# A decoder layer on one core: where the softmax's reciprocal and scaled copy stand in the order, when gathered rows are summed and normed, and how many constants' products run at the start

## The reference, cut to what matters

```python
def reference(x, ctx_1024, ...):            # x, ctx: (8, 256, 128)
    x = _layernorm(x + attention(x))        # sparse attention, 8 heads
    x = _layernorm(x + retention(x, ctx, ctx))   # 16 heads of 8
    return _layernorm(x + top2_moe(x))      # 8 experts, 128 -> 512 -> 128

# attention: index scores I choose 96 keys for each query (64 local, 32 chosen)
    _, idx = jax.lax.top_k(I, 96)
    scores = (einsum(q_c, k_c[idx]) + einsum(q_r, key_r)) * scale
    attn = softmax(scores)
    out = einsum('bhlk,bhlkd->bhld', attn, v[idx]) @ W_out
# retention: out = ((rot(Q) @ rot(K).T) * decay_mask) @ V
# moe:       hidden = relu(x @ w1 + b1);  all = hidden @ w2 + b2
#            y = sum over the two chosen experts of prob * all
```

## Time and profile before

| what | value |
|---|---|
| median of 3 executions | 669.03 us (668.65 to 680.7) |
| the profiled execution, its own time | 668.53 us |
| its span in the trace | 666.7 us |
| mean granted TensorE clock, of full speed | 0.961 |
| busy, share of the span | PE 88%, DVE 65%, ACT 61%, POOL 40% |

### The profile page before, as it was taken

The page is one execution under the profiler, slowest core; times in us unless marked ns, Lnnn a source line. Parts: engine busy times, 40 slices in busy tenths (PEclk is TensorE's granted clock), DMA queues, the critical chain, the costliest instruction groups (busy, mean ns, idle before and its releaser), DMA issues.

```text
span 666.7 us, 22154 instructions
## 1 busy us (share of the span) xinstructions
PE 585.0 (88%) x8225; PEld 439.7 (66%) x8225; DVE 432.2 (65%) x1618; ACT 406.9 (61%) x1381; POOL 268.0 (40%) x428
## 2 busy tenths in 40 slices
PE   5478988998898699999999898989997997789996
PEld 4244664665566367867787577757775677778886
DVE  0938848865976777578657976478657775333653
ACT  4437756674776657668765676377755665445352
POOL 1413912911570497017502898219304652005310
PEclk9869999999999969999999899799999999799999
DMA  5030153122014051543353435344262623886551
GB/s 170 2 123 14 28 189 133 22 63 84 19 24 137 14 162 27 188 157 108 107 156 117 130 80 174 99 154 116 66 206 77 189 67 100 242 241 196 166 160 44
DMA packets 58594, 75.86 MB, mean 114 GB/s; under 512 B 14256, under 2 KB 47480, under 8 KB 57336
## 3 DMA queue, kind: packets, MB, share of 16 engines
q1 hardware_dynamic: 56952, 71.30, 35.8%
q0 software_dynamic: 1536, 3.15, 1.6%
HBM read 58.92 MB, written 8.62 MB: 101 GB/s over the span
## 4 chain that ended last, share of the span: by engine, by line
PE 34%; POOL 11%; issue 9%; ACT 6%; DVE 4%; DMA 1%; SPq 0%; DVEq 0%; POOLq 0%; ACTq 0%
PE bW L1364 4%; PE bH L1299 3%; PE bR L1314 3%; PE bG L1083 3%; PE bM L920 3%; POOL gb L852 3%; PE bH L1350 2%; PE bG L1350 2%; ACT qV L1567 2%; PE bS L1102 2%; PE bM L1130 1%; PE bR L1222 1%; PE bM L1125 1%; POOL sorted_tokens L864 1%; POOL acc L895 1%
## 5 line engine op out<-in xcount | busy, mean ns | idle before, releaser
L1515 ACT ACTIVATE ppn<-pp,rls 128x224 f32<-128x224 f32 (+1 forms) x128 | 59.0, 461 | 34.0 <-DVE rls L1815 33.7
L1833 DVE TENSOR_TENSOR gs<-bG,rank_t 96x512 f32<-96x512 f32 x96 | 65.5, 682 | 15.0 <-PE bG L1083 13.8
L1507 ACT ACTIVATE pp<-pp,nmx 128x224 f32<-128x224 f32 x96 | 46.5, 484 | 31.1 <-DVE nmx L1826 30.2
L1896 DVE TENSOR_TENSOR sm<-bC,cst 128x512 f32<-128x512 f32 x64 | 43.6, 681 | 23.0 <-PE bC L1239 23.0
L1083 PE MATMUL bG<-oh,kspl 128*96 128x512 f32 x160 | 56.6, 435 | 0.0
L810 POOL TENSOR_TENSOR r<-x,cst 128x256 f32<-128x256 f32 x8 | 5.8, 725 | 123.0 <-DVE x L1860 123.0
L1826 DVE CUSTOM_DVE_ANT_0 pp<-bS,cst 128x224 f32<-128x224 f32 x96 | 36.3, 378 | 27.3 <-PE bS L1102 27.2
L1599 ACT ACTIVATE ht<-bH,wt 128x128 f32<-128x128 f32 x156 | 44.4, 370 | 14.5 <-PE bH L1299 14.5
L920 PE MATMUL bM<-cst,ppn 128*128 128x128 f32 (+1 forms) x224 | 47.8, 284 | 5.5 <-ACT ppn L1515 5.3
L1525 ACT COPY pts<-bM 128x256 f32<-128x256 f32 x96 | 35.4, 369 | 27.2 <-PE bM L920 26.3
L1299 PE MATMUL bH<-xt,wt 128*128 128x128 f32 x312 | 43.5, 284 | 3.0 <-DVE xt L2025 3.0
(11 more groups left out here) (296 smaller groups left out, 1644.8 us busy)
## 6 DMA issues: line engine op xcount, KB each, us to landing
wt<-in_experts SPq DMA_DIRECT2D x61, 578.0 KB, 4.0
sidx<-far_slots SPq DMA_DIRECT2D x8, 1536.0 KB, 6.9
vstk<-gs SPq DMA_DIRECT2D x96, 64.0 KB
xs<-sorted_tokens SPq DMA_DIRECT2D x45, 64.0 KB, 3.9
expert_rows<-ot SPq DMA_DIRECT2D x45, 64.0 KB, 3.7
sorted_tokens<-acc SPq DMA_DIRECT2D x9, 256.0 KB, 2.9
cst<-shape_constants SPq DMA_DIRECT2D x1, 1595.5 KB, 6.3
xn<-in_x SPq DMA_DIRECT2D x8, 128.0 KB, 3.3
```

The lines of the kernel that those rows point to most:

```text
L1507: AC(pp[:, s % 2, 0:w], bS[:, 0:w] if s < T0 else pp[:, s % 2, :], ACT.Exp, scale=1.0 if s < T0 else -1.0, bias=nmx[:, s % 2:s % 2 + 1], a ...
L1515: AC(ppn[:, t % 2, 0:w], pp[:, t % 2, 0:w], ACT.Copy, scale=rls[:, t % 2:t % 2 + 1]).then_inc(s_nrm.sem, 1)
L1833: TT(gs[:, g % 2, :].rearrange("p (t j) -> p t j", j=FAR), bG[0:96, :].rearrange("p (t j) -> p t j", j=FAR), rank_t[:, :].rearrange("p (o ...
L1896: free(TT(sm[:, u % 4, :].rearrange("p (v c) -> p v c", v=4), bC[:, :].rearrange("p (v c) -> p v c", v=4), C("causal").rearrange("p (o c) ...
```

## The change

Three things are altered.

First, for turns 3 to 15 DVE's reciprocal stands at s+0.25 in place of s+0.75, and ACT's scaled copy at the end of s+0.25 in place of s+0.75. Turns 0 to 2 stay as they were.

Second, of the six constants' products at the start of step 0 four are gone: slots 0 and 2 had two each and have one, slot 1 had two and has none. The other steps' stay.

Third, the table of gathered rows: the spacing of the two batches is 2 slots in place of 3, the sum comes 3 slots after the gather in place of 4, the mean 6 in place of 7 and the norm 7 in place of 9. That is gather in slots 7 and 9, sum 10 and 12, mean 13 and 15, norm 14 and 16.

```diff
--- before.py
+++ after.py
@@ -70,8 +70,9 @@
 TILE_SLOTS = (0, 2, 4, 5, 8, 10, 13, 15, 17)
 LIST_SLOT, FIRST_SLOT = 2, 6
 FILLED = ((2,), (1, 2))
+FILLS_FIRST, FILLS = 1, 2
 FETCH_SLOTS = (4, 5, 6)
-SUM_LATE, MEAN_LATE, NORM_LATE = 4, 7, 9
+SUM_LATE, MEAN_LATE, NORM_LATE = 3, 6, 7
 END_SLOTS = (0, 1, 2, 3, 4, 5, 6, 7, 8, 9, 9.5, 10, 11)
 DENSE_SLOTS = (11.5, 12, 13, 14, 15, 16, 17, 18, 19)
 
@@ -90,7 +91,7 @@
         g = GROUP_OF[n]
         if g < LAST:
             step, s = ends[g]
-            s += 2 + 3 * (n - GROUPS[g][0][0])
+            s += 2 + 2 * (n - GROUPS[g][0][0])
             for table, late in ((gather, 0), (first, SUM_LATE), (second, MEAN_LATE), (third, NORM_LATE)):
                 table[step + (s + late) // NS, (s + late) % NS] = n
     return at, gather, first, second, third
@@ -1139,14 +1140,14 @@
                 if s == 0:
                     pe.wait_ge(a_free.sem, a_free.at(i.n, 15))
                 if s == int(s):
-                    if s in FILLED[i.n <= GROUPS[0][0][-1] + 1]:
-                        fill(2)
+                    if s in FILLED[0 < i.n <= GROUPS[0][0][-1] + 1]:
+                        fill(FILLS_FIRST if i.first else FILLS)
                     if s < NT:
                         scores(i, s)
                     if T0 <= s + 1 < NT:
                         gather(i, s + 1)
                     if s == 0:
-                        fill(2)
+                        fill(FILLS_FIRST if i.first else FILLS)
                     return
                 if s > int(s) + 0.25:
                     return
@@ -1494,6 +1495,12 @@
                         dst = qall[:, p, 1024 * t:1024 * t + 1024].rearrange("p (t h) -> p h t", h=NH)[:, 4 * hg:4 * hg + 4, :]
                         free(copy(dst, ring(u)[:, :].rearrange("p (h t) -> p h t", h=4)))
 
+            def divide(i, t):
+
+                w = 96 if t < T0 else SW
+                act.wait_ge(s_rec.sem, s_rec.at(i.n, t + 1))
+                AC(ppn[:, t % 2, 0:w], pp[:, t % 2, 0:w], ACT.Copy, scale=rls[:, t % 2:t % 2 + 1]).then_inc(s_nrm.sem, 1)
+
             def stage_b(s, i):
                 p = i.par
                 if s < 0:
@@ -1507,12 +1514,8 @@
                         AC(pp[:, s % 2, 0:w], bS[:, 0:w] if s < T0 else pp[:, s % 2, :], ACT.Exp, scale=1.0 if s < T0 else -1.0,
                            bias=nmx[:, s % 2:s % 2 + 1], accum_out=lsum[:, s % 2:s % 2 + 1]).then_inc(s_exp.sem, 1)
                     return
-                if s == int(s) + 0.75 and s < NT:
-
-                    t = int(s)
-                    w = 96 if t < T0 else SW
-                    act.wait_ge(s_rec.sem, s_rec.at(i.n, t + 1))
-                    AC(ppn[:, t % 2, 0:w], pp[:, t % 2, 0:w], ACT.Copy, scale=rls[:, t % 2:t % 2 + 1]).then_inc(s_nrm.sem, 1)
+                if s == int(s) + 0.75 and s < T0 - 1:
+                    divide(i, int(s))
                 if s > int(s) + 0.25:
                     return
                 s = int(s)
@@ -1533,6 +1536,8 @@
                             act.wait_ge(c_full.sem, c_full.at(i.n - 1, C_AT["out"] + 1))
                         last = copy(ots[:, :, TQ * t:TQ * t + TQ], bM[:, WEIGHED:WEIGHED + 32].rearrange("p (a q) -> p a q", a=2))
                     last.then_inc(m_out.sem, 1)
+                if T0 - 1 <= s < NT:
+                    divide(i, s)
 
             def rsqrt_start(i, k):
 
@@ -1790,10 +1795,17 @@
                         top_keys(i)
                         ranks()
 
+            def inverse(i, t):
+
+                dve.wait_ge(s_exp.sem, s_exp.at(i.n, t + 1))
+                nc.vector.reciprocal(rls[:, t % 2:t % 2 + 1], lsum[:, t % 2:t % 2 + 1]).then_inc(s_rec.sem, 1)
+
             def stage_b(s, i):
                 p = i.par
                 if s < 0:
                     return
+                if s == int(s) + 0.25 and T0 - 1 <= s < NT:
+                    inverse(i, int(s))
                 if s in (1.25, 3.25, 5.25, 7.25, 9.25, 11.25):
                     s = int(s)
 
@@ -1808,11 +1820,8 @@
                         last = TS(oh[:, c % 2, 1, :], src, C("key_no")[:, 2:3], None, ALU.is_equal)
                     last.then_inc(o_ready.sem, 1)
                     return
-                if s == int(s) + 0.75 and s < NT:
-
-                    t = int(s)
-                    dve.wait_ge(s_exp.sem, s_exp.at(i.n, t + 1))
-                    nc.vector.reciprocal(rls[:, t % 2:t % 2 + 1], lsum[:, t % 2:t % 2 + 1]).then_inc(s_rec.sem, 1)
+                if s == int(s) + 0.75 and s < T0 - 1:
+                    inverse(i, int(s))
                 if s != int(s):
                     return
                 if s < NT:
```

## The result

The changed kernel took 675.23 us in the median of four executions (673.53 to 686.73), the kernel before 668.84 us (665.47 to 680.7) in the same comparison. The ratio is 1.0103, with an interval of 1.0061 to 1.0145: about 1% slower. The profiled execution took 673.53 us, its span 671.7 against 666.7.

What follows compares the result with a forecast made beforehand. It took PE, 88% busy, as the bound, hardly waiting for the hurried result. From 668.5 us, −2.9 + 6.9 + 1.2 + 2.4 − 1.2 + 1.5 − 4.6 + 3.3 = +6.6 gave 675.1, stated as 675.0, range 660 to 683.

Steps and rivals of the forecast that it cites:

- Bound, and what the change pushes back: PE hardly waits for the hurried scaled copy (5.3 us; −1.2 gained) but waits 8.3 for the masked product sm, pushed back.
- Slot 3, +6.9: Reciprocal passes one-hot and masked product; DVE stands still for ACT's sum, delaying PE in steps 1 to 7: +6.9 us.
- Slots 5 and 7, +1.2: Same one-hots passed; 0.3 us in each of two slots in steps 1 and 2, +1.2 us (0 to 4).
- Slot 15, +2.4: Reciprocal passes the keys' split; PE waits 0.8 us more in each of steps 0, 1 and 2, +2.4 us.
- Constants' products, −2.9: Start of step 0: four products gone save 3.6 us, a later clock rise takes 0.7 back; bounds −1.0 and −4.5.
- Step 5, +1.5: Gathered rows: batch 1's sum on POOL delays rotated keys and split; step 6's queries gain; net +1.5 us (0 to +3.5).
- GpSimd beside VectorE: Step 5: by the shared-interface rule, DVE's split beside POOL's scaling would be slow, adding 1.2 us to the 2.3 taken.
- Step 8, −4.6: Gathered rows, steps 7 and 8: PE's waits for xt, rotated queries and expert's weights shrink, −4.6 us (0 to −7).
- Clock, +3.3: Two new PE waits of 1.95 us, steps 4 and 6, each followed by a lower-clock stretch costing 1.7: +3.3 us.
- Rival 1: PE's later waits take up the waits for the exponential's sum: 661.3 us, faster by 1%; chance 0.26.
- Rival 2: New gaps in slot 3 bring long low-clock stretches, over 2% slower, 692.6 us with all four; chance 0.08.
- Rival 3: Gathered rows give nothing in step 8, PE there waiting for DVE's second layernorm chain anyway: 679.7 us; chance 0.12.

Runs made afterwards that it cites:

- fills_only: Only the four constants' products removed, against the kernel before: 666.5 us, ratio 1.0022 (0.9978 to 1.0067).
- whole_again: The whole change measured once more on a third chip, against the kernel before: 700.68 us, ratio 1.0169 (1.0121 to 1.0218).
- recip_gather: Early reciprocal and scaled copy plus the new gathered rows' table, all six constants' products kept, against the kernel before, third chip: 699.47 us, ratio 1.0159.
- recip_unpassed: Reciprocal and scaled copy early only in turns 4, 6, 12, 13 and 14, against the kernel before: 665.77 us, ratio 0.9979 (0.9949 to 1.0008).
- gather_only: Only the table of gathered rows changed, against the kernel before: 663.07 us, ratio 0.9936 (0.9897 to 0.9976).
- recip_only: Only the first part, reciprocal and scaled copy of turns 3 to 15 early, against the kernel before: 682.6 us, ratio 1.0246 (1.0202 to 1.0289).
- recip_dve_only: DVE's reciprocal early in turns 3 to 15, ACT's scaled copy at its old place, against the kernel before, second chip: ratio 1.0335 (1.0263 to 1.0407).

## Why the prediction was right

Forecast 675.0, measured 675.23. The mechanism of the largest term, slot 3, and the direct waits of slot 15 are right place by place, and so is the sign of the sum. That the sum meets the time to 0.2 us is luck: the products were forecast to gain and gained nothing that can be told, step 5 was forecast to lose and gained, slots 5 and 7 were put too low, and no clock was charged behind slot 15; these errors offset. On the third chip the same change cost 1.7% (1.0121 to 1.0218), which leaves out the 1.0% of the forecast. The terms one by one, by the profiles of the two kernels:

- **Bound, and what the change pushes back.** Right: PE's wait for ppn shrinks by 0.8 us (forecast 1.2 of gain), PE's wait for sm grows by 6.4 (forecast to about 14, it is 14.7). The two waits of 0.39 and 0.38 are the ones gone; the ones of 0.26, from which the other 0.4 of the forecast may come, are for turn 2, which keeps its place, and stayed.
- **Slot 3, +6.9.** Right place by place: steps 1 and 2 from 0.47 to 1.52 each (+1.05, forecast 1.0), steps 4 and 6 from none to 1.86 (forecast 1.95), step 7 from 1.49 to 2.25 (+0.76, forecast 0.7), steps 3 and 5 from 2.86 to 2.92 and from 1.70 to 1.92 (forecast 0.15 each). Sum +6.9. Later waits in steps 1 and 2 gave back some of it: the next wait for sm went from 0.71 to 0.42 in step 1 and from 0.65 to 0.42 in step 2.
- **Slots 5 and 7, +1.2.** Too small. In turn 7 the wait passes through one-hot and sm on to the maximum of turn 8, and PE waits for that: 0.89 and 0.88 us in steps 1 and 2, 0.79 in step 5; nmx in all 4.3 more. Turn 7 alone costs 8 us (2 to 14). The term was sized by a third of slot 3 instead of following DVE's queue to the next maximum.
- **Slot 15, +2.4.** Waits +0.81 in each of three steps, as forecast, and none in steps 3 to 7. The clock behind them had not been charged; in the changed kernel's profile step 1 begins 2.6 us later against turn 15 of step 0, and the clock was at 0.50 from 91 to 97 us. Turn 15 alone costs 9 us (5.7 to 12.7).
- **Constants' products, −2.9.** The step that failed. The timed runs show nothing (*fills_only* 1.0022, *whole_again* against *recip_gather* +0.1%), and their interval leaves out 2.9 us of gain. The sum took 3.6 us of PE's work as saved and 0.7 back for a later rise of the clock. In the changed kernel turn 2 came 1.6 us earlier than in before's profile in place of 2.9, but kernels with all six products have turn 1 anywhere from 2.1 earlier to 4.3 later, by when the clock rose. What the clock takes back was therefore not to be read from one profile, and it stays open. The Trainium skill's rule ("Perfetto Trace Analysis", section Matmul Optimizations: power follows utilization, so matmuls should run back to back) spoke for the lower bound, −1.0, and the timed result is nearer to that. The windows 44:46 and 46:48 of *fills_only* and of before agree with the rule, at 0.50 without the products and 0.98 and 1.00 with them; *recip_unpassed*, full before the first product, and *gather_only*, at 0.50 until after 50 us with all of them, do not show it.
- **Step 5, +1.5.** Wrong in sign. PE's wait for the split there is gone in the changed kernel (0.27 us, for kS). Turn 11 came 12.7 us later than before, while POOL's sum of batch 0 came only 6.3 later, so POOL had caught up: rkn was done at 421.8, 4.1 us before the sum of turn 15, and the split ran at 425.97, behind the reciprocal, in 0.79 and 0.69 us. Where POOL hadn't caught up, *gather_only* has 1.21, less than the 2.01 of the earlier trace rows and more than the 0.94 of *fills_only*. With rqn of step 6, also forecast in this term, every kernel with the new table gains about 1.2 net at turns 1 to 3 of step 6 (8.0 to 6.7 in the changed kernel's differences; without the table they stay flat).
- **GpSimd beside VectorE.** By the rule of the Trainium skill ("GPSIMD Engine Reference", section Key points: the two share SBUF interfaces, with contention where VectorE's instruction has two SBUF inputs) the prediction reckoned that the split would be as slow beside POOL's scaling as beside its sum. *gather_only* put the two side by side:

```profile
424.46 2.19 POOL L895 TENSOR_SCALAR acc<-acc,fmv,fln 128x128 f32<-128x128 f32 x2
...
424.50 0.69 DVE L1735 TENSOR_TENSOR rks<-rkn,high 128x512 uint32<-128x512 uint32 x1 [0.98 <-POOL rkn L815]
425.23 0.74 DVE L1737 TENSOR_TENSOR rks<-rkn,rks 128x512 f32<-128x512 f32 x1
```

DVE's two halves took 0.69 and 0.74, hardly more than the 0.69 each of step 2, so the 1.2 us did not come. It was POOL that took longer, 2.19 us in place of the 1.57 of the next two scalings in the same profile. Beside POOL's sum the split was slow again, 1.52 and 1.10 in *recip_unpassed* as before, and there the last two operations of the sum took longer too, 1.05 and 1.06 in place of 0.73 each. So the traces agree with the rule that the two contend, at both places; who pays differed, and no run shows by what it is decided.
- **Step 8, −4.6.** Measured −4.7: from 9.7 us late at turn 15 of step 7 to 5.0 at the end. The waits give 3.5 of it (2.84 + 1.82 + 1.83 to 1.48 + 0.28 + 1.26), the clock at 1.00 in place of 0.57 the rest, less a wait of 1.10 for qV behind them. The same difference is −2.8, −2.5, −1.3 and −3.7 in the four other profiles with the new table and −0.5 to +1.6 in the eight others without it, so the place is right and the size at the upper end.
- **Clock, +3.3.** The mean granted clock fell from 0.961 to 0.956. Low stretches appear behind the new waits at 89, 309 and 454 us, two of them in steps 4 and 6 as forecast, and the one at 416 is gone: 13.0 us late at turn 15 of step 5 and 8.0 at turn 0 of step 6. That gain of 5 is also in *fills_only* (4.6) and *recip_only* (4.5), but only 1.0 of it in *recip_unpassed*, which has the wait and the stretch too. It goes with POOL having caught up, in eleven profiles of fourteen. How often the kernel before has it without the change isn't known, so how much of the 5 us is an effect of the change stays open. The prediction had no such term.

Rival 1 (waits taken up) fell: *recip_only* was 16 us slower, not equal. Rival 2 (long low stretches) didn't come on the chip of the measurement; on chips with a lower clock the first part, whole or DVE's half of it, cost 3.2 to 3.4% in place of 2.5%, with intervals that overlap, so its mechanism may be in that, not shown. Rival 3 fell with the waits of step 8, and rival 4 with the loss of *recip_only*.

The first part alone was expected at +12.6 by my terms and took 15.7, the third at −3.1 and took −4.3, the second at −2.9 and took +1.5 (no different from nothing). Their sum by my terms is 6.6, by their own measurements 13, and the whole gave 6.4 on one chip and about 12 on another. The intervals allow some of that; the rest is what stays open on how parts add.

## What to carry to other kernels

Moving a waiting instruction up in an in-order queue helps its own reader and holds back everything that it passes. So look at what each passed instruction's readers wait for; here the reader on PE of the hurried result waited 5.3 us in all and those of the passed ones 8.3. Moved only in turns where nothing is passed, the reciprocal cost nothing and gained nothing that can be told; moved in all, it cost 2.5%. Follow the delay to the next thing in the queue, not only to the first. What a single profile shows at one place may differ in the next execution: before a wait or a shift of some microseconds carries a term, look at the same place in the profiles of kernels that are equal up to there. The shift of 1.5 us at the start looked like the products' effect until it stood beside kernels that had kept all six.

## What the runs showed of the hardware

The granted clock rose to full at the start of step 0 at about 38 us in two profiles of kernels that are the same up to there, at about 42 in four, at 44 in one, and at about 53 in two; turn 1 moved with it, from 2.1 us earlier to 4.3 later. In a tenth, *recip_dve_only*, the record of the clock reads 1.00 all along, but the block of slot 0 took 3.67 us, as at the lower level (1.91 at the upper), so this record isn't to be trusted there. Low stretches moved about too: behind the keys' split of step 5 there was one in the profile of before and in *recip_unpassed*, with waits of 2.01 and 2.09, and none in *fills_only*, with 0.94. Waits of the same length had a stretch behind them in one place and none in another: 1.66 us at 155.16 had one, 1.66 at 218.15 in the same execution had none. Two DVE operations of 0.69 us each took 1.52 and 1.10 beside POOL's sum and 0.69 and 0.74 beside its scaling, which itself took 2.19 in place of 1.57. The same kernel on another chip took 689 in place of 667 us with a lower granted clock, and the first part of the change cost 3.2% on a third chip (1.0275 to 1.0371) in place of 2.5% (1.0202 to 1.0289).
